# Folding the steering's partial sums in two rounded products in place of one float32 product

## What is computed

```python
U_o = gram_schmidt(U)                       # 512 x 32
V_o = gram_schmidt(V)
basis = U_o @ V_o.T
strength = (base_act * mod * knob)[:, None, :]
proj = hidden_states @ basis
feats = proj @ basis.T[:, :R]               # R = 32
response = feats @ resp_w.T + resp_b + safety_bias
return hidden_states + strength * response
```

## Time and profile before

| | us |
|---|---|
| median of 3 runs | 1609.07 |
| lowest, highest run | 1608.97, 1609.23 |
| profiled execution, first to last instruction | 1610.9 |
| busy: TensorE matmul | 1585.8 (98%) |
| busy: TensorE weight load | 1299.5 (81%) |
| busy: VectorE | 1166.6 (72%) |
| busy: ScalarE | 982.8 (61%) |
| busy: GpSimd | 410.9 (26%) |

### The profile page before, as it was taken

The page is one execution under the profiler, slowest core; times in us unless marked ns, Lnnn a source line. Parts: engine busy times, 40 slices in busy tenths (PEclk is TensorE's granted clock), DMA queues, the critical chain, the costliest instruction groups (busy, mean ns, idle before and its releaser), DMA issues.

```text
span 1610.9 us, 27177 instructions
## 1 busy us (share of the span) xinstructions
PE 1585.8 (98%) x9296; PEld 1299.5 (81%) x9298; DVE 1166.6 (72%) x2767; ACT 982.8 (61%) x2331; POOL 410.9 (26%) x605
## 2 busy tenths in 40 slices
PE   7999999999999999999999999999999999999999
PEld 4688786777777777777777688898999999999998
DVE  7999888786969686868778576785655656565643
ACT  6888766887878787878778755352433324242422
POOL 8998810313222313131312110201010110202010
PEclk8999999999999999999999999999999999999999
DMA  7042135543545444444337435866464555556361
GB/s 308 0 183 97 66 126 126 149 130 92 138 95 139 100 115 122 111 116 115 88 90 214 167 152 207 303 262 232 178 234 170 213 225 188 212 178 265 142 211 68
DMA packets 62257, 254.79 MB, mean 158 GB/s; under 512 B 10628, under 2 KB 16004, under 8 KB 46760
## 3 DMA queue, kind: packets, MB, share of 16 engines
q1 hardware_dynamic: 62120, 253.06, 48.2%
HBM read 153.93 MB, written 48.23 MB: 125 GB/s over the span
## 4 chain that ended last, share of the span: by engine, by line
PE 90%; POOL 3%; DMA 2%; DVE 2%; ACT 1%; issue 1%; SPq 1%; POOLq 0%; DVEq 0%; ACTq 0%
PE psum L83 24%; PE psum L84 23%; PE psum L85 23%; PE psum L1529 5%; PE psum L1549 5%; PE psum L1579 4%; PE psum L1470 1%; DMA k_weights<-w_factors 1%; PE psum L1478 1%; PE psum L2451 1%; DMA k_raw<-in_t_w 1%; POOL k_gs_square L252 1%; POOL k_gs_root L247 1%; ACT psum L1229 1%; POOL k_gs_scaled L256 1%
## 5 line engine op out<-in xcount | busy, mean ns | idle before, releaser
L1229 ACT ACTIVATE psum<-psum,b_mx 128x512 f32<-128x512 f32 (+3 forms) x512 | 258.9, 509 | 63.2 <-DVE b_mx L990 62.0
L990 DVE CUSTOM_DVE_ANT_0 psum<-psum,b_mask 128x512 f32<-128x512 f32 (+3 forms) x512 | 244.7, 506 | 53.0 <-PE psum L1529 48.1
L2398 ACT ACTIVATE k_act<-k_stack_f,k_smalls 128x512 f32<-128x512 f32 x112 | 80.9, 722 | 303.6 <-DVE k_stack_f L2237 297.1
L1241 ACT ACTIVATE k_exps<-psum 128x512 f32<-128x512 f32 (+1 forms) x384 | 194.6, 532 | 59.4 <-PE psum L1549 58.1
L864 POOL TENSOR_SCALAR_AFFINE_SELECT k_exps<-k_exps 128x256 f32<-128x256 f32 x256 | 96.4, 413 | 381.0 <-ACT k_exps L1241 379.1
L2097 POOL TENSOR_SCALAR k_result<-k_result,k_pb 128x512 f32<-128x512 f32 x32 | 59.2, 1866 | 434.9 <-DVE k_result L2156 434.9
L2216 DVE TENSOR_TENSOR k_act_lo<-k_act,k_act_hi 128x512 fp32r<-128x512 f32 x112 | 77.2, 690 | 120.6 <-ACT k_act_hi L2401 120.6
L83 PE MATMUL psum<-k_act_hi,k_w_hi 128*128 128x512 f32 x384 | 150.8, 393 | 0.0
L84 PE MATMUL psum<-k_act_lo,k_w_hi 128*128 128x512 f32 x384 | 150.5, 392 | 0.0
L85 PE MATMUL psum<-k_act_hi,k_w_lo 128*128 128x512 f32 x384 | 150.2, 391 | 0.0
L2237 DVE TENSOR_TENSOR k_raw<-psum,k_raw 128x256 f32<-128x256 f32 x168 | 70.5, 421 | 106.0 <-PE psum L85 95.4
(11 more groups left out here) (372 smaller groups left out, 4418.2 us busy)
## 6 DMA issues: line engine op xcount, KB each, us to landing
k_stack<-w_factors SPq DMA_DIRECT2D x35, 1792.0 KB, 7.7
k_stack<-k_samples SPq DMA_DIRECT2D x384, 128.0 KB, 2.4
k_weights<-w_factors SPq DMA_DIRECT2D x17, 1792.0 KB, 7.5
x<-k_tokens SPq DMA_DIRECT2D x10, 1024.0 KB, 4.3
k_tokens<-x SPq DMA_DIRECT2D x8, 1024.0 KB, 5.1
d<-k_result SPq DMA_DIRECT2D x32, 256.0 KB, 2.9
k_raw<-x SPq DMA_DIRECT2D x8, 1024.0 KB, 4.8
k_raw<-d SPq DMA_DIRECT2D x8, 1024.0 KB, 7.1
```

Source lines behind the costliest of these rows:

```text
L990: last = dve.tensor_tensor_reduce(got, got, mask[:, S - width:S], -INV_SQRT_DH, -2.0 * MASKED, ALU.add, ALU.min, mx[n % 2][:, h, t:t + 1])
L1229: act.activation(sc(n, u)[:, at:at + width], sc(n, u)[:, at:at + width], ACT.Exp, bias=mx[n % 2][:, h, t:t + 1], scale=-1.0, accum_out=sum ...
L1241: act.activation(exps[n % 2][:, h, at:at + width], by_key(n, u)[:, 0:width], ACT.Exp, scale=INV_SQRT_DH).then_inc(k_act, 1)
L2398: act.activation(act_f[:], whole_tile, ACT.Gelu, bias=small(smalls, "b1", 2 * pair % M + second)).then_inc(pair_gelu, 1)
```

## The change

The fold reads its operand as a rounded high part and a remainder, both float32r, in two products that add up in one bank. The identities in `fold` are float32r too. For this

- ScalarE's copy writes the rounded type into `psb` itself and counts up `p_hi`, not `pj_act`;
- a new step on VectorE, `parts_rest`, waits for that copy (and for the split of the sample before, `xl_set`), subtracts the rounded part from the bank and writes the remainder, 128x512, into memory of the token buffer that is free then (`token_sums`); it is now the step that says that the bank has been taken;
- `p_folded` waits for it and makes two products;
- the counts of `p_hi` in `p_low` grow, since two copies for each sample count there now;
- `parts_rest` stands in VectorE's order behind `values_out(0, 0)` for sample 1, behind `max_unit(3, 8)` for sample 2, and in the loop behind `max_unit(n + 1, 8)`, before `maxima_out(n + 1, 0)`.

```diff
-TAKEN_BY = {"st": "dve", ..., "tb": "act", "pt": "act"}
+TAKEN_BY = {"st": "dve", ..., "tb": "act", "pt": "dve"}
...
-    uo, fold, steer = sb("uo", [P, J, R]), sb("fold", [P, 3, R]), sb("steer", [3 * R + 2, J, P], F32R)
+    uo, fold, steer = sb("uo", [P, J, R]), sb("fold", [P, 3, R], F32R), sb("steer", [3 * R + 2, J, P], F32R)
...
-    parts = nc.alloc_sbuf_tensor_at("b_p_parts", [P, S], F32, offset=psb_at)
+    parts_low = keep["token_sums"][:, 0, :]
...
+        def parts_rest(b):
+            dve.wait_ge(p_hi, 2 * b)
+            dve.wait_ge(xl_set, J * b)
+            dve.tensor_tensor(parts_low, pj(("pt", b, 0)), psb[:].bitcast(F32), ALU.subtract).then_inc(pj_dve, 1)
+
         def p_low(b):
-            dve.wait_ge(p_hi, b + 1)
+            dve.wait_ge(p_hi, 2 * b + 1)
...
             max_unit(n + 1, 8)
+            if b + 2 < B:
+                parts_rest(b + 2)
             maxima_out(n + 1, 0)
...
         def p_parts(b):
             wait_full(act, ("pt", b, 0))
-            act.activation(parts[:], pj(("pt", b, 0)), ACT.Copy).then_inc(pj_act, 1)
+            act.activation(psb[:], pj(("pt", b, 0)), ACT.Copy).then_inc(p_hi, 1)
...
-            pe.matmul(out[0:3 * R, :], fold[:].rearrange("p k r -> p (k r)"), parts[:], start=True,
-                      stop=True).then_inc(pj_full, 1)
+            pe.matmul(out[0:3 * R, :], fold[:].rearrange("p k r -> p (k r)"), psb[:], start=True, stop=False)
+            pe.matmul(out[0:3 * R, :], fold[:].rearrange("p k r -> p (k r)"), parts_low, start=False, stop=True).then_inc(pj_full, 1)
...
     att.values_out(0, 0)
+    att.parts_rest(1)
...
     att.max_unit(3, 8)
+    att.parts_rest(2)
     att.maxima_out(3, 0)
...
+        keep["token_sums"] = nc.alloc_sbuf_tensor_at("k_token_sums", [P, 2, S], F32R, offset=at + 4 * (J + 1) * S)
```

More of the change, by code:

```diff
@@ L609 @@
 V_TILES = ((0, 1), (3, 2))
-TAKEN_BY = {"st": "dve", "q": "dve", "k": "dve", "v": "dve", "wo": "dve", "p": "dve", "tin": "act", "tb": "act", "pt": "act"}
+TAKEN_BY = {"st": "dve", "q": "dve", "k": "dve", "v": "dve", "wo": "dve", "p": "dve", "tin": "act", "tb": "act", "pt": "dve"}
 BANK_ORDER = (
@@ L683, in attention_engines @@
     high_at = lambda n: ch[:, n % (G + 1), :] if n % (G + 1) < G else ch_last[:]
-    psb_at = aligned(nc.sbuf_base)
     psb = sb("p", [P, S], F32R)
-    parts = nc.alloc_sbuf_tensor_at("b_p_parts", [P, S], F32, offset=psb_at)
+    parts_low = keep["token_sums"][:, 0, :]
     mask = sb("mask", [P, S])
@@ L1187, in slots @@
                 both[n // 2 % 2](n, n // G)
-        return steps(gate_constants, row_high, row_low, head, strengths, coefficients, steering, p_low, steered, statistics, normalise, weight_low, split_low, result_constants,
+        return steps(gate_constants, row_high, row_low, head, strengths, coefficients, steering, parts_rest, p_low, steered, statistics, normalise, weight_low, split_low, result_constants,
                      qk_out, values_out, max_unit, shift_rows, maxima_out, ctx_low, attention_result, wo_low, first_sum, slots)
```

## The result

The changed kernel took 1613.41 us (median of 20 runs, 1610.74 to 1617.94) against 1609.21 us before on the same chip (20 runs, 1607.35 to 1614.7). The medians lie 4.2 us apart. The ratio of the two sets of runs is 1.0021 with a 95% interval of 1.0013 to 1.003, so 2.1 to 4.8 us slower, 3.4 in the middle. The forecast of 3.0 us more lies inside that, and 1613.41 lies inside the forecast's range of 1606.3 to 1614.3. That alone says little about the reasons; the trace has to show them.

The account below looks back on a forecast made before the run. TensorE, with 90% of the chain and short handovers between engines, was taken to bound the kernel. 0 + 0.1 + 2.9 gave +3.0 us on the median 1609.07: 1612.1, range 1606.3 to 1614.3.

Parts of the forecast that it names:

- Part 1: TensorE's fold: one float32 product of 0.88 us becomes two rounded ones of 0.23, 0.42 less each, seven times 2.9.
- Part 2: ScalarE's copy out of PSUM stays at 0.60 us though it now writes the rounded type; cost 0.
- Part 3: New subtraction on VectorE, seven times: about 0.68 us, beginning at 645.00 to 645.10 and ending at 645.68 to 645.78.
- Part 4: TensorE's wait for the subtraction before the fold's products eats the 0.42 us saved: break even, or 0.1 lost.
- Part 5: Work queued behind VectorE's subtraction: row maximum 0.97 to 1.07 us late, exponential 0.6 to 0.75; 0.58 a sample, 2.9 total.
- what TensorE gets back: After the late exponential, TensorE recovers a tenth or so of its 0.6 to 0.75 us where it next waits for ScalarE.
- SyncE's transfers: Transfers of the maxima and the stack go out about 1.0 us later; cost to TensorE 0 to 0.2, taken as 0.
- Samples 1 and 2: Folds in the hand-written head: the first sample costs 0, the second 0.1 us.
- Clean gain: Rival: subtraction done before TensorE asks, late maximum harmless; five to seven times 0.42 us less, 1606.2 to 1607.0; chance 0.12.
- Break even through small waits: Rival: the delay queued behind the subtraction goes into small waits no row shows; 1609.1 to 1610.6 us; chance 0.16.
- The whole delay passes: Rival: maxima's transfers or row maxima reach TensorE with the full 1.0 us a sample; 1614.2 us; chance 0.15.
- Not doing what it says: Rival: a rounded product costs 0.44 us, so 0.42 more each on top of the wait; 1614.1 us; chance 0.03.

Follow-up runs that it names:

- e_no_sub: Changed kernel without the subtraction, both products reading the rounded part: 1610.46 us, ratio to the kernel before 1.0003 (0.9994 to 1.0012).
- e_sub_only: Kernel before, keeping its float32 product, with an unused subtraction added on VectorE in the change's place: 1612.43 us, ratio 1.0013 (1.0004 to 1.0022).
- after_again: The changed kernel run and profiled once more, unedited: 1613.70 us, ratio to the kernel before 1.0017 (1.0008 to 1.0027).
- e_dve_late: Changed kernel with the subtraction moved behind row maximum 9 on VectorE, both products still waiting for it: 1621.31 us, one run.

## Why the prediction was right, and where not

**What bounds the kernel.** Right as far as it went: TensorE's chain and short handovers between three engines. But TensorE's chain hid a second thing: it was already waiting for ScalarE right behind the fold. In e_no_sub the saving turned into waits of 0.26 and 0.28. The earlier trace rows showed 0.17 of the second; of the first it showed nothing.

**Part 1, 0.42 less.** Right: the second product starts 0.23 behind the first where nothing makes it wait, as at sample 1:

```profile
250.63 0.39 PE L1456 MATMUL psum<-b_p,b_fold 128*96 128x512 f32 x1
250.86 0.40 PE L1457 MATMUL psum<-k_token_sums,b_fold 128*96 128x512 f32 x1
```

The 131 ns of the Trainium skill (TensorE: Matmul & The Clock Gate, section Back-to-back issue gap) don't appear for this pair; the measurement decides, as the forecast took it. **Part 2, the copy**: 0.60 in both, right.

**Part 3, the subtraction.** 0.69 forecast as 0.68. Its start, 644.96, was forecast as 645.00 to 645.10: the handover between ScalarE and VectorE was 0.03, below the 0.06 to 0.16 taken from other pairs.

**Part 4, break even.** The balance is right, 0.00 at the product at 646.84, but it came about otherwise: TensorE waited 0.25, not 0.4 to 0.5, and the fold started 0.28 late, not 0.42 to 0.52, as 0.17 from a release to a product was too much (0.04 in the chain). In return the first product shows 0.47, so the two took 0.70 in the chain, not 0.46.

**Part 5, the queue behind.** The mechanism is right and proved by e_sub_only: row maximum, exponential, score product. **The mis-sized terms** are these. The row maximum was 0.86 late, not 0.97 to 1.07: 0.04 to 0.14 from the earlier start of the subtraction, 0.08 from the maxima's step starting ahead of the subtraction's end. ScalarE had 0.33 to spare, forecast as 0.30, so its exponential was 0.53 late, not 0.6 to 0.75. And what TensorE gets back was 0.19, not "a tenth or so". The product at 647.54 was forecast 0.4 to 0.55 late and was 0.28. What TensorE gets back was mis-sized because I read idle time of TensorE from its products, where overlapping records hide it; the weight load at 653.95 had the gap of 0.23 in the trace of before. 0.53, which grows to 0.56 on the way, less 0.19 is 0.37. TensorE comes out of the two score products 0.53 late, where 0.6 to 0.75 was forecast. The idle time that was to show it didn't keep its size either: 0.34 on ScalarE for 0.6 to 0.75, 0.25 on TensorE at the fold for 0.4 to 0.5.

SyncE's transfers cost 0 in the loop: no trace has a wait of TensorE for them there. But all the traces with the subtraction in the loop have one such wait behind it, of 0.41 to 0.89 us, and the five without it have none:

```profile
867.06 0.19 PEld L1555 LDWEIGHTS psum<-k_stack 98*128 98x128 f32 x1 [0.48 <-DMA k_stack<-k_maxima]
```

The forecast knew nothing of it. It leaves nothing that lasts: at the wait for the weights, some 170 us on, TensorE is 0.29 and 0.35 late, no more than sample 7's fold alone costs.

**Samples 1 and 2.** Sample 1 as forecast, 0: TensorE is 2.44 later than before both ahead of the fold and behind the wait for k_v, which is still there (the 2.44 go with the clock at the start: its mean over 20 to 30 us was 0.99 in the trace of before and 0.73 in this one, and 0.98 in after_again, which is 0.28 later there):

```profile
251.74 0.19 PEld L83 LDWEIGHTS psum<-k_normed,k_weights 128*128 128x128 f32 x1 [0.49 <-DVE k_v L1021]
```

Sample 2: TensorE is 0.97 later ahead of the fold and 1.20 behind it, so 0.23, not 0.1. (In between, 259.2 to 262.4, the trace of before ran at 0.50 of full speed, and this one didn't.) But the 0.23 doesn't repeat: counted from its partial sums, the first q and k product behind this fold comes after 4.14 in both traces of before, 4.33 in the first of the changed kernel and 4.13 in the second. The subtraction came at 315.27, later by 0.4 than forecast from the earlier trace rows once the 0.97 is taken off.

**The sum.** By the traces 5 x 0.37 is 1.9 us, and with the 0.23 of the first trace 2.1, not 3.0. The many runs gave 2.1 to 4.8 and 1.3 to 4.3 for the changed kernel, and 0.6 to 3.5 for e_sub_only. 2.1 is at the low edge of the first and within the other two. So the total agreed better than the terms deserve, and that is partly luck. Compared at the same clock the changed kernel takes 1.0 to 1.1 longer from sample 7's partial sums to the end (885.10 against 884.08, 886.26 against 885.12). Of that 0.29 and 0.35 arise ahead of the wait for the weights; the rest is the length of that wait, 2.31 against 1.64 and 1.69 against 0.73. Two traces of each can't tell whether the change makes it longer on the average, so the distance between 2.1 and the 3.4 in the middle of the interval stays open. I forecast the sign by steps that hold, with the lateness too large and the slack too small.

**The rivals.** Clean gain: false, e_no_sub has 0.07 a sample even without the subtraction. Break even through small waits: half true, it is what took 0.33 and then 0.19. The whole delay passes: false here, but e_dve_late shows it where the wait stands on TensorE itself. Not doing what it says: false.

## What to carry to other kernels

Before shortening a product, look for the next wait of its engine behind it: the saving is worth no more than the distance to the latest of these, here 0.07 of 0.42. A step added to an engine in a tight chain costs its lateness less the idle time of each engine that it runs through, so a place a few instructions on can be worth more than the step's own length, but only if its consumer moves as well: moving the subtraction alone cost 0.5 more, moving both saved 0.21. Look for the slack of TensorE in the gaps between weight loads, which the overlapping records of the products hide, and then test it: here one of 0.23 was worth 0.19, one of 0.16 only 0.04. And before reading single spans, compare the granted clock and the long waits for transfers in both traces.

## What the runs showed of the hardware

- Handover between engines varied by pair: from ScalarE's copy to VectorE's subtraction 0.03 us, from VectorE's subtraction to TensorE's weight load 0.04 in the chain, where the earlier trace rows had 0.06 from ScalarE to TensorE.
- A product that is released by another engine has a longer record than one that stands in a row: 0.47 against 0.39 us for the same form at L1456. In the first case its record starts together with that of its weight load, both at 648.13; at sample 1 it starts 0.22 behind it (250.41 and 250.63). So the longer record holds the time of the weight load.
- VectorE's subtraction of two 128x512 operands took 0.69, over 256 columns 0.42: halving the columns took off 0.27, not half.
- The granted clock fell from 2.4 to 1.2 GHz in one execution and not in another of the same kernel at the same place, behind the same 2.79 of 4 us of TensorE's work. The fall cost 1.6 to 1.7 us.
